# First self attention: the decay as a difference of running sums instead of a product with the triangle in every step

## The reference

```python
q = (hidden_states @ Wq).reshape(B, T, H * R, D)     # H = 8 groups, R = 2 query heads each
k = (hidden_states @ Wk).reshape(B, T, H, D)
v = (hidden_states @ Wv).reshape(B, T, H, D)
log_g = jax.nn.log_sigmoid(GATE_OFFSET + g)          # g = hidden_states @ Wg: one per position and group
logG = jnp.cumsum(log_g, axis=1)                     # running sum along the sequence
a = (einsum('bthd,bshd->bhts', q, k) * scale) ** 2
gate = logG[:, :, :, None] - logG[:, :, None, :]     # logG[t] - logG[s]
a = jnp.where(causal, a * jnp.exp(gate), 0.0)
norm = jnp.sum(a, axis=-1) + 1e-06
y = jnp.einsum('bhts,bshd->bthd', a, v) / norm
return y.reshape(B, T, H * R * D) @ Wc + bc
```

## Time and profile before

| | us |
|---|---|
| median of 3 runs | 2582.27 |
| lowest and highest run | 2581.72, 2593.28 |
| the profiled execution, its own time | 2584.34 |
| its span, first to last instruction | 2582.6 |

### The profile page before, as it was taken

One profiled execution on the slowest core, in us unless ns is written; L12 is line 12 of the kernel. 1 busy time (PEld: TensorE's weight loads), 2 busy tenths in 40 slices (PEclk: granted clock), 3 DMA queues, 4 the chain that ended last, 5 costly groups with the idle time before them and its releaser, 6 DMA issues. The chain is left out here.

```text
span 2582.6 us, 38373 instructions
## 1 busy us (share of the span) xinstructions
PE 2235.2 (87%) x14368; PEld 1799.7 (70%) x14368; DVE 1204.0 (47%) x3113; ACT 981.8 (38%) x2234; POOL 679.0 (26%) x693
## 2 busy tenths in 40 slices
PE   5999999999998688878999999858898847888774
PEld 3989988988987466666888877656565436767542
DVE  2343333343335566655111113336777745677656
ACT  2222222222222466633121111223655635777632
POOL 2442332332231121112343410023443331332110
PEclk8999999999999767789999999887999868999886
DMA  5000000000000110010010000023332130000001
GB/s 191 1 29 13 9 29 13 9 21 13 9 1 1 64 44 26 1 54 33 25 50 17 17 1 1 1 49 53 51 54 49 28 114 13 14 26 10 1 9 65
DMA packets 34631, 78.08 MB, mean 30 GB/s; under 512 B 5264, under 2 KB 17680, under 8 KB 31504
## 3 DMA queue, kind: packets, MB, share of 16 engines
q1 hardware_dynamic: 34448, 75.63, 10.4%
HBM read 55.16 MB, written 4.19 MB: 23 GB/s over the span
## 5 line engine op out<-in xcount | busy, mean ns | idle before, releaser
L1108 PE MATMUL PS<-WH,bXH 128*128 128x512 f32 x512 | 200.9, 392 | 5.4 <-POOL WL L1385 5.4
L1108 PE MATMUL PS<-WL,bXH 128*128 128x512 f32 x512 | 200.4, 391 | 0.0
L1108 PE MATMUL PS<-WH,bXL 128*128 128x512 f32 x512 | 200.4, 391 | 0.0
L558 DVE TENSOR_TENSOR xN<-PS,xN 128x512 f32<-128x512 f32 x128 | 88.5, 691 | 228.0 <-PE PS L361 228.0
L1790 DVE TENSOR_REDUCE aM<-PS 128x4 f32<-128x1024 f32 x128 | 155.0, 1221 | 52.1 <-PE PS L1630 51.1
L1303 DVE SCALAR_TENSOR_TENSOR s<-s,cf,PS 128x256 f32<-128x256 f32 x112 | 53.8, 480 | 249.1 <-ACT s L1223 240.1
L1733 ACT ACTIVATE aPT<-PS 128x1024 f32<-128x1024 f32 x128 | 129.4, 1024 | 69.8 <-PE PS L1650 68.5
L1223 ACT ACTIVATE s<-PS 128x256 f32<-128x256 f32 x128 | 49.0, 383 | 277.3 <-PE PS L1108 277.3
L330 PE MATMUL PS<-aXH,QKH 128*128 128x512 f32 x384 | 152.3, 397 | 0.0
L643 POOL TENSOR_TENSOR E<-E,DM 128x256 f32<-128x256 f32 x64 | 47.1, 736 | 392.4 <-ACT E L475 392.4
L330 PE MATMUL PS<-aXH,QKL 128*128 128x512 f32 x384 | 149.6, 390 | 0.0
(11 more groups left out here) (405 smaller groups left out, 6264.1 us busy)
## 6 DMA issues: line engine op xcount, KB each, us to landing
sg<-in_gu SPq DMA_DIRECT2D x8, 1024.0 KB, 4.9
aqs<-aQH SPq DMA_DIRECT2D x64, 128.0 KB, 4.2
gQK<-in_Wqk SPq DMA_DIRECT2D x8, 768.0 KB, 4.2
V<-in_xT SPq DMA_DIRECT2D x4, 1024.0 KB, 6.3
gC<-in_Wc SPq DMA_DIRECT2D x8, 512.0 KB, 3.6
xN<-in_x SPq DMA_DIRECT2D x4, 1024.0 KB, 8.7
cst<-in_cT SPq DMA_DIRECT2D x8, 512.0 KB, 4.8
cV<-in_c SPq DMA_DIRECT2D x8, 512.0 KB, 4.0
```

The source lines that it names most:

```text
L558: e.tensor_tensor(xN[:, t, :], PS[:, b, :], xN[:, t, :], ALU.add).then_inc(o_add.sem, 1)
L1108: mm = e.matmul(PS[:, b, :], x[:, kc, 128 * t:128 * t + 128], w[:, kc, :], start=kc == 0 and i == 0, stop=kc == KC - 1 and i == 2)
```

## The change

The triangle product goes out of the step. Once, after `project(0)`, PE makes the running sums of all 16 tiles and 8 groups at a time (`gate_sums`): `UT` times `lg`, and ones times the even tiles added to the odd ones, so that the sum runs through a sequence of 256. DVE copies them to `lgS` (position on the partitions), PE transposes them, DVE copies the result to `lgR` (position along the row), SP writes `lgR` to DRAM, and from there each step's 512 sums come back as one row over all 128 partitions, `lgB`, with two buffers. In each step POOL computes `E` = min(lgB - lgS, 0) in two instructions for each j, ACT takes the exponential in place, and POOL multiplies by `DM` as before.

```diff
-        A = W("A", [128, 2, 3, 128])
+        lgS, lgR, lgB = W("lgS", [128, NT * 8]), W("lgR", [128, 128]), W("lgB", [128, 2, 512])
+    rows = nc.dram_tensor("gate_sums", [8, 2048], F32, kind="Internal").ap()
@@ banks
-            for j in (0, 1):
-                R.use(("gate", n, j), 1, e_exp.upto(2 * n + j + 1))
+            if n == 0:
+                R.use("sums", 1, sum_out.upto(1))
+                R.use("turned", 1, sum_rows.upto(1))
@@ PE, project(n)
-            for j in (0, 1):
-                ...
-                e.wait_ge(*a_in.upto(2 * n + j + 1))
-                e.matmul(PS[:, b, 0:128], A[:, j, 0, :], UT[:, 0:128], ...)
-                e.matmul(PS[:, b, 128:256], A[:, j, 0, :], UT[:, 128:256], ...)
-                e.matmul(PS[:, b, 128:256], A[:, j, 1, :], UT[:, 0:128], ...)
-                e.matmul(PS[:, b, 256:384], A[:, j, 2, :], UT[:, 0:128], ...).then_inc(e_mm.sem, 1)
+        def gate_sums():
+            ...
+            e.wait_ge(*gates.upto(1))
+            e.matmul(PS[:, b, 0:128], UT[:, :], lg[:, :], start=True, stop=False, skip_group_check=True)
+            e.matmul(odd, K.onesF[:, :], even, start=False, stop=True, ...).then_inc(sum_mm.sem, 1)
+        def gate_rows():
+            ...
+            e.wait_ge(*sum_out.upto(1))
+            e.transpose(PS[:, b, 0:128], lgS[:, :], idF[:, :]).then_inc(sum_turned.sem, 1)
@@ PE, loop over n
                 project(n)
+            if n == 0:
+                gate_sums()
+                gate_rows()
@@ ACT, project(n), behind the copies of q
-                if n:
-                    e.wait_ge(*s_at.upto(2 * n - 1 + j))
-                e.wait_ge(*e_mm.upto(2 * n + j + 1))
-                e.activation(E[:, j, :], PS[:, b, 0:384], ACTF.Exp).then_inc(e_exp.sem, 1)
+                e.wait_ge(*e_diff.upto(2 * n + j + 1))
+                e.activation(E[:, j, :], E[:, j, :], ACTF.Exp).then_inc(e_exp.sem, 1)
@@ DVE, n == 0, behind the copy of k
+            e.wait_ge(*sum_mm.upto(1))
+            e.tensor_copy(lgS[:, :], PS[:, rooms["sums"][0], 0:128]).then_inc(sum_out.sem, 1)
+            e.wait_ge(*sum_turned.upto(1))
+            e.tensor_copy(lgR[:, :], PS[:, rooms["turned"][0], 0:128]).then_inc(sum_rows.sem, 1)
@@ POOL
-        e.wait_ge(*gates.upto(1))
+        e.wait_ge(*sum_out.upto(1))
...
+                    if j == 0:
+                        e.wait_ge(*rows_in[n % 2].upto(n // 2 + 1))
                     if n:
-                        e.wait_ge(*e_mm.upto(2 * n - 1 + j))
-                    e.tensor_scalar(A[:, j, 0, :], MSK[:, :], lg[:, c0:c0 + 1], None, ALU.mult)
-                    e.tensor_scalar(A[:, j, 1, :], K.onesF[:, :], lg[:, c1:c1 + 1], None, ALU.mult)
-                    e.tensor_scalar(A[:, j, 2, :], MSK[:, :], lg[:, c1:c1 + 1], None, ALU.mult).then_inc(a_in.sem, 1)
+                        e.wait_ge(*s_at.upto(2 * n - 1 + j))
+                    e.tensor_scalar(E[:, j, 0:256], lgB[:, n % 2, 256 * j:256 * j + 256], lgS[:, c0:c0 + 1], 0.0,
+                                    ALU.subtract, ALU.min)
+                    e.tensor_scalar(E[:, j, 256:384], lgB[:, n % 2, 256 * j + 128:256 * j + 256], lgS[:, c1:c1 + 1],
+                                    0.0, ALU.subtract, ALU.min).then_inc(e_diff.sem, 1)
@@ SP
+        e.wait_ge(*sum_rows.upto(1))
+        e.dma_start(rows.rearrange("g (t q) -> t g q", q=128), lgR[:, :]).then_inc(rows_out.sem, 16)
+        e.wait_ge(*rows_out.upto(1))
+        def gate_rows(n):
+            g, p = steps[n]
+            if n >= 2:
+                e.wait_ge(*e_diff.upto(2 * n - 2))
+            e.dma_start(lgB[:, n % 2, :], rows[g:g + 1, 512 * p:512 * p + 512].broadcast_to([128, 512])).then_inc(
+                rows_in[n % 2].sem, 16)
+        gate_rows(0)
+        gate_rows(1)
@@ SP, loop over n, behind the load of gQK and ahead of those of xN, gC and gV
+            if 1 <= n < N - 1:
+                gate_rows(n + 1)
```

More of the change, by code:

```diff
@@ L234, in attention0 @@
         wg, wgH, wgL = W("wg", [128, KC, 8]), W("wgH", [128, KC, 8], F32R), W("wgL", [128, KC, 8], F32R)
-        MSK, UT, DM = W("MSK", [128, 128]), W("UT", [128, 256]), W("DM", [128, 2, 128])
+        UT, DM = W("UT", [128, 128]), W("DM", [128, 2, 128])
+        lgS, lgR, lgB = W("lgS", [128, NT * 8]), W("lgR", [128, 128]), W("lgB", [128, 2, 512])
         bc = W("bc", [128, 512])
@@ L255, in attention0 @@
     qk_mm, q_out, k_out = K.flag("pe_qk", 3 * N), K.flag("act_q", 2 * N), K.flag("dve_q", N)
-    a_in, e_mm, e_exp, e_in = K.flag("pool_gate_rows", 2 * N), K.flag("pe_gate", 2 * N), K.flag("act_gate", 2 * N), K.flag("pool_gate", 2 * N)
+    sum_mm, sum_out, sum_turned, sum_rows = (K.flag(f, 1) for f in ("pe_gate_sums", "dve_gate_sums", "pe_gate_turned", "dve_gate_rows"))
+    rows_out, rows_in = K.dma("dma_gate_rows"), (K.dma("dma_gates0", N // 2), K.dma("dma_gates1", N // 2))
+    e_diff, e_exp, e_in = K.flag("pool_gate_diff", 2 * N), K.flag("act_gate", 2 * N), K.flag("pool_gate", 2 * N)
     s_mm, s_sq, s_at = K.flag("pe_scores", 2 * N), K.flag("act_square", 2 * N), K.flag("dve_powers", 2 * N)
@@ L332, in project @@
                 mm.then_inc(qk_mm.sem, 1)
-            for j in (0, 1):
[L334 to L338, removed]
-                e.wait_ge(*a_in.upto(2 * n + j + 1))
[L340 to L346, removed]
+        def gate_sums():
+            b, left = rooms["sums"]
+            for w in left:
+                e.wait_ge(*w)
+            e.wait_ge(*masks.upto(1))
+            e.wait_ge(*gates.upto(1))
+            e.matmul(PS[:, b, 0:128], UT[:, :], lg[:, :], start=True, stop=False, skip_group_check=True)
+            odd = PS[:, b, 0:128].rearrange("p (a c g) -> p a c g", c=2, g=8)[:, :, 1, :]
+            even = lg[:, :].rearrange("p (a c g) -> p a c g", c=2, g=8)[:, :, 0, :]
+            e.matmul(odd, K.onesF[:, :], even, start=False, stop=True, skip_group_check=True).then_inc(sum_mm.sem, 1)
+        def gate_rows():
+            b, left = rooms["turned"]
+            for w in left:
+                e.wait_ge(*w)
+            e.wait_ge(*sum_out.upto(1))
+            e.transpose(PS[:, b, 0:128], lgS[:, :], idF[:, :]).then_inc(sum_turned.sem, 1)
         def out(n):
@@ L612, in gpsimd @@
         step = K.steps(e, "pool_step")
-        e.memset(MSK[:, :], 1.0)
         e.memset(UT[:, :], 1.0)
         step(e.memset(DM[:, :, :], 1.0))
-        e.affine_select(out=MSK[:, :], in_=MSK[:, :], compare_op=ALU.is_gt, fill=0.0, base=0, pattern=[[-1, 128]],
-                        channel_multiplier=1)
-        e.affine_select(out=UT[:, 0:128], in_=UT[:, 0:128], compare_op=ALU.is_ge, fill=0.0, base=0,
+        e.affine_select(out=UT[:, :], in_=UT[:, :], compare_op=ALU.is_ge, fill=0.0, base=0,
                         pattern=[[1, 128]], channel_multiplier=-1)
```

1 line of the change is left out of this document (removed).

## The result

The changed kernel takes 2525.4 us, the median of four runs (2507.3 to 2531.2), against 2583.0 us of the kernel before in the same session (2581.7 to 2593.3). The ratio is 0.9746, with an interval of 0.9712 to 0.9780: faster, by 57 to 74 us. (The two medians alone give 0.9777, at the edge of that interval.) A second session gave 2528.5 us (2511.1 to 2540.8, six runs) and 0.9805 (0.9757 to 0.9853): clear of no change, but on both sides of a gain of 2%. Runs more than 1.5% above the fastest of their kernel count as slow and stand in no ratio: one of the ten of experiment 1, and three of the 17 of the kernel before beside it. The forecast was 2524, with a range from 2518 to 2539; the ratio puts the time at 0.9746 x 2583.0 = 2517.4, just under the range, while the median lies in it.

A forecast was written before the change was run, and what follows sets the result against it. PE's saturated stream bounds the first self attention: 53.7 + 1.7 + 2.95 = 58.3 us saved takes the profiled 2584.3 to 2526.0, and 2524 as median, since the profile lies 2.1 above it. Range 2518 to 2539.

The forecast's parts named there:

- The price of a product: PE, first self attention: removing eight triangle products and a format change saves 1.79 us in 30 steps, 1.70 in step 1.
- Step 0: Start of the first self attention: 5.65 us go, 1.3 of new work and charges of 0.9 and 0.5 leave 2.95.
- 0.9 for the clock: Step 0: PE's clock loss may fall on values(0), between nothing and 1.7 us; half was charged.
- 0.5 for tile 8: Step 0: PE may wait for its bank at V tile 8, behind ACT's late copies; 0.5 us charged, bounds 0 and 14.
- The chain that ends in the V copies: Step 0: lgB at 59, then POOL's differences, ACT's exponential and tile 0's copy, ending 63.5 against tile 8 at 64.4.
- POOL: Each attention step: four differences take 3.6 us, bounds 2.7 and 7.9, hidden by about 8 us of slack.
- DMA, banks, DVE, ACT, SP: Attention steps: row loads, bank reuse, DVE delays up to 1.35 us, ACT's reads and SP's 32 loads cost nothing.
- The prediction's other estimate: DMA at the start: about 2.0 us fixed plus bytes over 436 GB/s, 4.8 us for both transfers against 5.7 by rows.
- The first rival: The start is exposed: slow transfers and differences make PE wait 13.8 us at tile 8; 2539, half of it 2531; chance 0.10.
- third rival: The loop through E becomes the step: at 6 us per difference the kernel is slower, 2672 us; chance 0.03.
- the second: Rival: each step gives the gain back, DVE and POOL disturbing each other until yL misses out; 2570 to 2582; chance 0.05.
- later stages meeting the clock otherwise by 2 or 3: Stages behind the first attention: a different granted clock moves the time by 2 or 3 us, part of the range 2519 to 2531.

The follow-up runs named there:

- experiment 1: Changed kernel with the eight triangle products put back on PE as idle work in every step but step 0: 2574.4 us, ratio 0.9965.
- experiment 4: Changed kernel with POOL forming each difference twice, the extra one into a scratch tile: 2529.05 us in one run.
- experiment 3: Changed kernel with the first 1 MB residual load issued ahead of the first two row loads, so lgB arrives later: 2529.6 us in one run.
- experiment 5: Changed kernel with POOL's differences done six times, five of them into BF16 scratch that nobody reads: 2770.2 us in one run.

## Why the prediction was nearly right, and where it failed

- **The price of a product: right.** 1.79 us forecast for each of 30 steps and 1.70 for step 1; measured 1.80 in steps 2 to 30 and 1.79 in step 1. (0.32 less 0.22, the prediction's own rows, are 0.10 and not 0.09 for the format change.) Experiment 1 gives all of it back and nothing else.
- **Step 0: mis-sized.** I had 2.95 us; it gave 4.56 in the pair of profiles. Two terms were charged that did not occur: 0.9 for the clock (1.00 granted; PE's gap shrank to 0.5 us, and in none of the ten traces with that gap did the clock fall behind it) and 0.5 for tile 8. The chain that ends in the V copies was forecast to end at 63.5 with tile 8 at 64.4; it stood at 63.4 (the copy's start, 62.99, and the 0.41 from a copy's start to PE's in experiment 4) with tile 8 at 64.1, so 0.7 us were left. Experiments 3 and 4 show the edge from its other side. The kernel before has its 2.0 us wait in all six traces without the change, and what comes of it differs: step 0 is 38.8 us in the two where the clock stays up, and 39.8 (two, the profile of before among them) or 41.5 us (two) where it falls to 1.2 GHz behind the wait, for a shorter or a longer stretch. In the changed kernel it is 35.1 to 35.2. So this term gives 3.6, 4.6 or 6.4 us by the clock of the kernel before, which the prediction took as fixed. Over the six traces without the change the stage ends at 852.4 to 857.4 (mean 854.8), over the six with it (experiments 1 and 3 to 5 left out) it ends at 793.9 to 796.3 (mean 795.0): 59.8 us between the means.
- **POOL: right in what follows, 0.6 us off in size.** 4.2 us a step, forecast 3.6. That `aT` would take 2.3 us beside the differences was wrong; in step 0, beside POOL's VL, it does (2.31), as before. The Trainium skill ("GPSIMD Engine Reference", Specifications) has VectorE's instructions with two SBUF inputs contend with GpSimd; the runs agree that they do, but show GpSimd's one-input difference as the one that pays.
- **DMA, banks, DVE, ACT, SP: free, right.** 3.7 and 2.1 us against 3.1 and 2.6 by the rows. The prediction's other estimate, from the Trainium skill ("DMA: Bandwidth & Descriptors", Anatomy of one DMA), 2.6 and 2.15, fits the write and is 1.1 us short for the row; that section is on transfers that GpSimd issues, while SP issues these.
- **The rivals' sizes.** The first rival has its place and its prices right, as experiment 4 shows; its edge was 0.7 to 0.9 us away. The contention between VectorE and GpSimd, which the prediction lays to its third rival, bears on the second. The lower bound of -2 for step 0 follows from none of the terms given.
- **The step that failed: "later stages meeting the clock otherwise by 2 or 3".** The stages behind the attention have the same instructions, but the first cross attention is 251 to 265 us long in two traces of the kernel before and 256 to 259 in two of the changed one, and the second attention moves by 4 to 7 more. Those are some 10 us either way, for which the own range, 2519 to 2531, left 2 or 3; one of the four first runs took 2507.3. The ratio's 2517.4 lies 0.6 us under the range, a small part of that. I had the runs of before to see it by: three of them already spread over 12 us, and the row of windows over the cross attention would have shown a granted clock of 0.73:

```profile
854.70:1105.90 251.20, 204.58 (x1792) 157.35 (x1793) 162.32 (x677) 152.47 (x588) 47.83 (x34) 0.73 0.11 35
```

The mechanism stood. That the median came within 1.4 us of 2524 is in part luck: the attention gave 2.0 us more than the sum, the stages behind it took 1.4 back in that trace, and the runs spread over 24. The low end of the range was too high by what the clock there does.

## What to carry to other kernels

In a stretch where the windows show one engine busy for all of its time at a steady clock, an instruction taken out is worth its pitch there (from one start to the next, not its recorded duration), and what it costs elsewhere can be read as slack. Before giving a range, look at the granted clock of the stages that the change doesn't touch: where it is between the two levels, the same instructions take another time in each execution, and that, not the edit, sets the range. There it can pay to add work: one or two idle products ahead of a wait took 16 and 21 us off a stage of the changed kernel, while four took only 7 off, and the fastest kernel here (2505 to 2508 us) is the changed one with them.

## What the runs showed of the hardware

- The lower level of TensorE's clock (1.2 GHz) held for 123 to 195 us of the first cross attention in the ten traces without extra products, for 27 to 34 us in the three with two.
- POOL's difference (one tensor, two operations) takes 1.14 us for 256 columns and 0.71 for 128, beside DVE's two-input product 1.19. DVE's `aT` takes 0.96 beside it, and 2.31 beside POOL's two-input VL.
- After a wait of 2.5 us PE's pitch was 0.21 us instead of 0.12; after one of 1.7 us (experiment 3) and after those of 0.5 us the clock stood at 1.00. After the same 2.0 us wait of the kernels without the change it fell in four of six traces.
